# Context attention and layer kernel: prologue in another order, W turned in it, residuals in three steps, VectorE splits the layer's first three units

## The reference

```python
# 1: attention to the context, one W for queries and output
trans_q = einsum('bqh,oh->bqo', ctx, W) + b
att = softmax(einsum('bph,bqh->bpq', layernorm(x), trans_q))
x = x + relu(einsum('bph,oh->bpo', einsum('bpq,bqh->bph', att, ctx), W) + b)
# 2: a layer of linear attention (wq, wk, wv, wo, 16 heads) and a gelu MLP
# 3: a mixture of 8 gated experts, two of them for each token
```

## Time and profile before

| | us |
|---|---|
| runs | 699.74, 931.4, 698.71 (median 699.74) |
| profiled execution, its own time | 702.32 |
| its span, first to last instruction | 700.6 |
| TensorE busy | 651.6 |
| VectorE busy | 426.5 |
| ScalarE busy | 372.8 |
| POOL busy | 252.9 |
| mean granted TensorE clock | 0.968 |

### The profile page before, as it was taken

How to read it: one execution, slowest core, us unless ns; L and a number is a source line. 1 busy time by engine, 2 the same in 40 slices (tenths; PEclk the granted TensorE clock), 3 DMA queues, 4 the chain that set the end, 5 groups by cost and what they waited for, 6 DMA issues and landing times.

```text
span 700.6 us, 9558 instructions
## 1 busy us (share of the span) xinstructions
PE 651.6 (93%) x3370; PEld 538.0 (77%) x3371; DVE 426.5 (61%) x688; ACT 372.8 (53%) x523; POOL 252.9 (36%) x172
## 2 busy tenths in 40 slices
PE   4979998998998999989969999969999999999994
PEld 4868886886876788878758888768888888888883
DVE  8566666656677545576776354845475463762775
ACT  4499986986973254430142244322574555754850
POOL 5078885776894424340000022123022020220233
PEclk9999998998999999999989999969999999999998
DMA  8435453343041612221080793316599191991925
GB/s 324 187 120 175 148 182 129 121 138 118 9 143 60 198 61 90 83 98 62 1 279 22 242 403 120 120 46 238 182 353 373 53 360 46 356 371 66 341 84 176
DMA packets 51844, 116.95 MB, mean 167 GB/s; under 512 B 5208, under 2 KB 5208, under 8 KB 48736
## 3 DMA queue, kind: packets, MB, share of 16 engines
q1 hardware_dynamic: 47360, 106.51, 43.2%
q10 hardware_dynamic: 3168, 5.77, 2.4%
q0 software_dynamic: 1280, 4.20, 1.8%
HBM read 102.31 MB, written 14.16 MB: 166 GB/s over the span
## 4 chain that ended last, share of the span: by engine, by line
PE 78%; DVE 12%; ACT 3%; issue 3%; DMA 2%; POOL 1%; SPq 0%; POOLq 0%; DVEq 0%; ACTq 0%
PE bank L1351 18%; PE bank L1353 18%; PE bank L1352 18%; PE bank L1365 5%; PE bank L1416 3%; PE bank L1417 3%; PE bank L1384 3%; PE bank L1385 3%; PE bank L1750 1%; PE bank L1580 1%; PE bank L1401 1%; PE bank L1730 1%; PE bank L1568 1%; DVE xn L984 1%; PE bank L1737 1%
## 5 line engine op out<-in xcount | busy, mean ns | idle before, releaser
L466 POOL TENSOR_TENSOR nat_lo<-raw,nat_hi 128x512 fp32r<-128x512 f32 x104 | 134.3, 1315 | 55.9 <-ACT nat_hi L584 55.3
L515 POOL TENSOR_TENSOR e_lo<-e_raw,e_hi 128x2048 fp32r<-128x2048 f32 x9 | 41.6, 4619 | 230.2 <-ACT e_hi L743 230.2
L863 DVE TENSOR_TENSOR ct_lo<-bank,ct_hi 128x512 fp32r<-128x512 f32 x96 | 65.9, 689 | 48.7 <-ACT ct_hi L551 48.4
L1351 PE MATMUL bank<-w_hi,turned 128*128 128x512 f32 x176 | 70.7, 402 | 4.0 <-DVE turned L990 2.6
L551 ACT ACTIVATE ct_hi<-bank 128x512 fp32r<-128x512 f32 x96 | 57.1, 596 | 26.4 <-PE bank L1365 24.5
L1352 PE MATMUL bank<-w_lo,turned 128*128 128x512 f32 x176 | 69.5, 395 | 0.0
L1353 PE MATMUL bank<-w_hi,turned 128*128 128x512 f32 x176 | 69.4, 394 | 0.0
L584 ACT ACTIVATE nat_hi<-raw 128x512 fp32r<-128x512 f32 x104 | 65.0, 629 | 0.0
L1365 PE MATMUL bank<-ident,raw 128*128 128x128 f32 x384 | 61.1, 285 | 0.0
L1351 PE MATMUL bank<-e_hi,turned 128*128 128x512 f32 x144 | 59.0, 409 | 1.5 <-issue 1.5
L1365 PEld LDWEIGHTS bank<-ident,raw 128*128 128x128 f32 x384 | 50.1, 147 | 12.7 <-issue 1.2
(11 more groups left out here) (252 smaller groups left out, 1449.8 us busy)
## 6 DMA issues: line engine op xcount, KB each, us to landing
raw<-in_ctx_dram SPq DMA_DIRECT2D x24, 1024.0 KB, 5.0
w_raw<-in_L_ffn_w_dram SPq DMA_DIRECT2D x24, 1024.0 KB, 5.4
e_raw<-in_L_ffn_wo_dram SPq DMA_DIRECT2D x16, 1024.0 KB, 7.4
w_raw<-in_L_attn_w_dram SPq DMA_DIRECT2D x8, 1024.0 KB, 5.2
e_raw<-in_L_ffn_w_dram SPq DMA_DIRECT2D x8, 1024.0 KB, 7.4
slots_x<-zeros SPq DMA_DIRECT2D x1, 4096.0 KB, 16.9
slots_y<-zeros SPq DMA_DIRECT2D x1, 3840.0 KB, 26.2
vectors<-slots_x ACTq DMA_DIRECT2D x11, 256.0 KB, 5.0
```

Source lines behind the costliest of these rows:

```text
L466: nc.gpsimd.tensor_tensor(nat_lo[:, j, :], raw[b % 2][:, j, :], nat_hi[:, j, :].bitcast(f32), ALU.subtract).then_inc(nat_lo_ready, 1)
L515: nc.gpsimd.tensor_tensor(e_lo[j][:, :, :], e_raw[j][:, :, :], e_hi[j][:, :, :].bitcast(f32), ALU.subtract).then_inc(e_lo_ready[j], 1)
L863: nc.vector.tensor_tensor(ct_lo[:, n % CR, :], src, ct_hi[:, n % CR, :].bitcast(f32), ALU.subtract).then_inc(t_lo, 1)
L1351: nc.tensor.matmul(dst, lh, rh, start=first and k == 0, stop=False)
```

## The change

Four things, none of which changes what is computed.

1. The prologue's order. VectorE normalises the first two token tiles before the statistics of the fourth, and POOL waits for pn before its W_lo. TensorE does the first token product ahead of the first three context tiles, with its four W_hi x pnT_hi matmuls first.
2. W is turned between the token products, in bank VB[1] alone, and not in steps 4 to 10. The nat copies begin in step 8 instead of 6 and catch up with three in step 18 (values_at).
3. The residual is output_taken at its old step 41, the sum at step 45 and the statistics at 46 (after the batch pair's odd batch b, step 13 b + 41 and so on); for the third pair all of it comes after the loop.
4. Units 0, 1 and 2 are all split by VectorE, the first as the first thing behind the loop; value product 2 comes ahead of the turning of xn's third tile.

```diff
@@ rules and POOL
+        def values_at(s):
+            if s < 18:
+                return range(s - 8, s - 7) if s >= 8 else range(0)
+            return range(10, 13) if s == 18 else range(s - 6, min(s - 5, B * NKT))
...
+            pool.wait_ge(pn_ready, NT)
             for k in range(KD // 2, KD):
                 pool.wait_ge(W_hi_ready, k + 1)
...
-            split_w(1)
             first_roots(3)
-            split_w(2)
@@ ScalarE
-                if s in (4, 6, 8, 10):
-                    upper_WT(s // 2 - 2)
...
-                if 0 <= s - 6 < B * NKT:
-                    upper_values((s - 6) // NKT, (s - 6) % NKT)
+                for i in values_at(s):
+                    upper_values(i // NKT, i % NKT)
@@ VectorE, prologue
+            link(statistics((0, 1)))
+            variances(0)
+            last = statistics((2,))
+            tokens(0)
+            link(statistics((3,)))
+            variances(1)
+            lower_W(0)
+            tokens(1)
+            lower_W(1)
...
+            lower_pw(0)
             for n in range(3):
                 lower_context(n)
...
+            for m in range(1, KD):
+                lower_WT(m - 1)
+                lower_pw(m)
+                lower_context(2 + m)
+            lower_WT(KD - 1)
@@ VectorE, loop
-                    if b % 2 == 1 and s == G * b + (41 if b < B - 3 else 45):
+                    if b % 2 == 1 and b < B - 3 and s == G * b + 41:
+                        output_taken(b // 2)
+                    if b % 2 == 1 and b < B - 3 and s == G * b + 45:
                         residual(b // 2)
+                    if b % 2 == 1 and b < B - 3 and s == G * b + 46:
                         dve.wait_ge(x1_ready, b // 2 + 1)
                         first_stats(b // 2)
@@ VectorE, behind the loop
             split_w(0)
             lower_turned(0)
+            sum_values(B - 1)
             lower_turned(1)
-            sum_values(B - 1)
-            first_gained(2)
+            output_taken(NT - 2)
+            residual(NT - 2)
             lower_vectors(NT - 1)
+            dve.wait_ge(x1_ready, NT - 1)
+            first_stats(NT - 2)
+            split_w(1)
+            first_gained(NT - 2)
+            output_taken(NT - 1)
             residual(NT - 1)
...
+            split_w(2)
@@ TensorE
+            pe.wait_ge(pnT_hi_ready, NT)
+            pe.wait_ge(pnT_lo_ready, 1)
+            for k in range(KD):
+                pe.wait_ge(W_hi_ready, k + 1)
+                nc.tensor.matmul(bank[3][:, :], W_hi[:, k, 0:P], pnT_hi[:, k, :], start=k == 0, stop=False)
...
             for n in range(3):
                 context_turned(n)
...
+            for m in range(1, KD):
+                turned_W(m - 1)
+                token_product(m).then_inc(pwT_done, 1)
+                context_turned(2 + m)
+            turned_W(KD - 1)
...
             value_product(1)
             for k in range(KD):
                 projected_out(NT - 1, k)
+            value_product(2)
             tile_turned(2)
-            for n in range(2, 5):
+            for n in range(3, 5):
                 value_product(n)
```

More of the change, by code:

```diff
@@ L614, in upper_pn @@
                                      ACT.Copy).then_inc(pnT_hi_ready, 1)
-            for k in range(KD - 1):
-                upper_W(k)
+            upper_W(0)
+            upper_W(1)
             upper_pn(0)
-            upper_W(KD - 1)
-            for t in range(1, NT):
+            upper_W(2)
+            upper_pn(1)
+            upper_W(3)
+            for t in range(2, NT):
                 upper_pn(t)
+            upper_pw(0)
             for n in range(3):
                 upper_context(n)
-            upper_context(3)
-            upper_pw(0)
-            upper_context(4)
-            upper_pw(1)
-            upper_context(5)
-            upper_pw(2)
-            upper_pw(3)
+            for m in range(1, KD):
+                upper_WT(m - 1)
+                upper_pw(m)
+                upper_context(2 + m)
+            upper_WT(KD - 1)
             def split_w(u):
@@ L925, in bias_part, with statistics, variances @@
                     last.then_inc(pb_done, 1)
-            for half in range(2):
-                for t in (2 * half, 2 * half + 1):
+            def statistics(tiles):
+                for t in tiles:
                     dve.wait_ge(x_loaded[t], 16)
                     last = nc.vector.bn_stats(stats[:, t, :], xt[:, t, :])
-                link(last)
+                return last
+            def variances(half):
                 for t in (2 * half, 2 * half + 1):
@@ L1435, in turned_W, with token_product @@
             def turned_W(k):
-                pe.wait_ge(pw_lo_ready, KD)
-                if k >= 2:
-                    pe.wait_ge(WT_lo_ready, k - 1)
+                if k >= 1:
+                    pe.wait_ge(WT_lo_ready, k)
                 for m in range(KD):
-                    mm = nc.tensor.transpose(VB[k % 2][:, m * P:(m + 1) * P], Wn[:, m, k * P:(k + 1) * P], ident[:, :])
+                    mm = nc.tensor.transpose(VB[1][:, m * P:(m + 1) * P], Wn[:, m, k * P:(k + 1) * P], ident[:, :])
                 mm.then_inc(WT_done, 1)
+            def token_product(m):
+                return product(bank[3 + m][:, :], [(W_hi[:, k, m * P:(m + 1) * P], W_lo[:, k, m * P:(m + 1) * P]) for k in range(KD)],
+                               [(pnT_hi[:, k, :], pnT_lo[:, k, :]) for k in range(KD)])
             pe.wait_ge(const_ready, 1)
```

52 lines of the change are left out of this document (21 added, 31 removed).

## The result

| | before | changed |
|---|---|---|
| median of the runs | 699.23 us (698.71 without 931.4) | 690.87 us |
| runs | 697.96, 698.71, 699.74, 931.4 | 688.31, 689.71, 692.02, 692.91 |
| profiled execution: time, span | 702.32, 700.6 | 692.91, 691.1 |
| its granted clock, mean | 0.968 | 0.972 |

The ratio is 0.9884, with a 95% interval from 0.9845 to 0.9923. The change makes the kernel 1.2% faster (0.8 to 1.6%): 8.1 us by the ratio and 7.8 to 8.4 by the medians, where 17.8 were forecast. (The run of before at 931.4 us stands alone and is left out of the ratio; why it was slow is not known.)

A forecast was written before the change was run, and what follows sets the result against it. TensorE, busy 651.6 of 700.6 us, was taken as the bound, improvable only in idle and low-clock time. Gains 11.2 + 2.1 + 1.2 + 3.3 = 17.8 us gave 681.9 us, range 678 to 692.

The forecast's parts named there:

- Residual in three steps: In the batch loop: VectorE frees pT sooner, TensorE's two long waits fall to 0 to 0.3 us; gain 11.2 us.
- The second payment: In the batch loop: low-clock time behind each long pT wait, 3.1 of the 5.7 us that one wait costs.
- The base: Whole kernel: profiled 702.32 us less 17.8 gives 684.5; the median run lies 2.6 lower, so 681.9.
- Prologue and start of the loop: Before and in the first thirteen steps: score step 2.1 us earlier, then 1.2 us from three steps at the high level.
- its worse case: In the prologue: the first token product runs at the low level, taking 5.3 us instead of 2.8.
- The wait of 1.9 that was to stay: At the loop's start: TensorE still waits 1.9 us before its score step, with no clock fall behind it.
- the 1.2: At the loop's start: three steps take 3.3 us at the high level instead of 4.48; 0 if the level falls.
- Layer's first units: Behind the loop: VectorE splits unit 0 first and units 1 and 2 too; gain 3.3 us (1.5 to 4.5).
- the case in which VectorE issues first: Behind the loop: VectorE's unit 0 split gets in before POOL's last nat_lo, which ends at 211.6; gain 2.7 us.
- The second: Rival: start and tail give little (low-level first product, fall behind the remaining wait, VectorE first); gain 13.8, 685.9 us; chance 0.18.
- The first: Rival: the low level does not hang on the waits and comes elsewhere; only waits count, 8.8 us, 690.9 us; chance 0.12.
- the pace: Sign in the batch loop: the fourth and fifth batches' turnings lie 19.3 to 19.8 us apart.

The follow-up runs named there:

- e13: Kernel before with 9 products of a zero tile ahead of TensorE's pT waits in the fourth and sixth batch: 696.7 us, ratio 0.9969.
- e2: Kernel before with only the new start (statistics and token order, weight splits, first product, W turned in the prologue, natural values): 700.7 us, ratio 1.0003.
- e4: Changed kernel with the old start put back, residuals in three steps and new tail kept: 689.8 us, ratio 0.9854 to before.
- e6: Changed kernel with identity turnings added: 32 ahead of the first tokens, 8 between their pairs, 6 ahead of the first product: 686.3 us, ratio 0.9838 to before.
- e11: Changed kernel with ScalarE's natural values 2 to 5 moved to steps 12 and 13, two at a time: 691.8 us, ratio 0.9893 to before.
- e12: Changed kernel with warm start, ScalarE's unit 1 behind the last lower values, earlier first mask and later values 2 to 5: 681.9 us, ratio 0.9751 to before.
- e3: Kernel before with only the new tail (units 0 to 2, order of sums behind the loop, third value product): 698.7 us, ratio 0.9977.
- e8: Changed kernel with ScalarE's unit 1 split and its nat_lo wait behind the turned second tile and last lower values: 689.3 us, ratio 0.9866 to before.
- e14: e12 with identity turnings added, 26 ahead of the wait for the chosen experts, 12 ahead of the first expert's rows: 686.7 us, ratio 0.9816 to before.
- e5: Kernel before with 24 identity turnings in batches b = 4 and 6, behind the batches that wait for pT: 704.9 us, ratio 1.0076.

## Why the prediction was wrong

The sign and the mechanism of the largest term were right; all four terms were too large, and two of them came to nothing.

- **Residual in three steps, 11.2 us (ends 4.8 and 11.6): 6.9 alone.** This is the step that failed most, by 4.3 us, and it is a size. The three steps do free pT (waits of 2.6 us to none; fourth to fifth batch 19.6 us, as said), and each of the two waits did cost 2.5. The second payment, 3.1 us per wait, is what the profiled execution had; in the runs it is 1.1 on the mean (e13: 2.2 for both, interval 0.2 to 4.2). The sentence "so each long wait is paid twice" should have read: sometimes, and by different amounts.
- **The base.** 702.32 was carried to the median by taking off 2.6. But that execution lost more at the low level than most (22.4 us at a clock of 0.968, as much as the highest of the 21 runs of before above), and a part of that very loss was the gain that was forecast. It can't be won by the change and be left out of the base too.
- **Prologue and start of the loop, 2.1 + 1.2 us: nothing** (e2: 1.0003; e4). The loop began at 30.63, outside the 27.5 to 30.0. The first product ran at half the rate, which the prediction named as its worse case (5.3 us; it was 5.1) and did not take; e6 shows that this alone is 2.05 us, nearly all of the 2.1 that the loop was late. That it was still slow then is put down here to the gaps that the new order puts ahead of it (1.25 and 0.69 us), where before worked from 8.22 to 14.1 us without one; e6 filled the gaps and added 32 turnings ahead of the tokens at once, so this cause is argued and not shown apart. The wait of 1.9 that was to stay is 1.60, and behind it the level fell in five of the seven profiles that have it, so the 1.2 was mostly lost too (18.3 us from the loop's start to the first probabilities with the fall, 17.3 without). Where the wait is 0.66 (e11, e12) no fall followed.
- **Layer's first units, 3.3 us (4.1 or 2.7): 2.45** in the trace, 1.6 in the runs (e3, interval -0.5 to 3.7). VectorE got in first. Its split starts 0.07 us ahead of GpSimd's last subtraction, which takes 3.36 us, where its like in before took 1.29, and ends at 200.24; ScalarE, which waits for it, is late for the last lower values. By the rule of the Trainium skill, page "SBUF — State Buffer", section "Who interferes with whom", this is the case in which VectorE issues first, with 2.7, and the 3.36 agrees with it. No xn takes 5 us any more (1.67 at most), since GpSimd has no split beside it. That unit 1 would be in the way of the last sum on ScalarE was in the prediction's working, but not as something that an order could mend; e8 takes 1.4 us from it.
- **Rivals.** The second described the start and the tail as they came (low level through the first product, loop at 30.0 or later, a fall behind the wait that stays, VectorE first), but kept 11.2 for the residual and so named 685.9. The first named the very time, 690.9, but that is luck: its 8.8 us held 2.1 for the start, which gave nothing, and e13 speaks against its claim that the level doesn't hang on the waits, for the waits for pT. What it had right is that the level falls elsewhere too, at a place where before had shown none. That 690.9 lies within the range of 678 to 692 is owed to these two rivals alone; the forecast's own gains ended at 14, and a gain under 2% had a chance of 0.26.
- **What would show it.** Met: no 2.6 us for pT, the pace, 1.00 from 50 to 200 us, no xn of 5 us. Not met: the loop's start, the first probabilities (48.94, not 45.4), av only 1.7 us nearer the last probabilities. Neither condition for being wrong came true as it was written (no wait over 2.5 us at a new place, no low level in the batches from 50 to 200 us). What took 4.7 us in the profile was a place that neither looked at: 0.51 for 14 us in the attention, behind a wait of 1.42.

Open stays why the level falls in one execution and not in the next behind the same wait, and why all four runs of e11 lost over 17 us. Where the level fell in executions without a profile is not on record, only the sum over each.

## What to carry to other kernels

Split a gain into the wait, which every execution has, and the low clock behind it, which comes and goes: read the latter over several executions (span x (1 - clock) of each, as an upper bound), never from one profile. Before a first long product, and through a wait that can't be removed, turnings of the identity into a free bank are a cheap way to keep TensorE fast, but they help only if they fit: at a low level they outlast the wait and are late themselves (e14). And when an instruction that must wait stands on an in-order engine, look at what is queued behind it (here unit 1's split ahead of the last lower values) before counting what the new order gives.

## What the runs showed of the hardware

- The loss at the low level comes in steps: 1.7, 3.4 or 6.8 us at one place, whatever the wait. At the fourth batch's wait of 2.56 us it was 3.4 in before, 1.7 in e5 and 0 in e3, which run the same instructions up to there. Behind the wait of 2.54 to 2.58 us in the layer's start it was 1.7 in each of five profiles.
- At the start TensorE works at half its rate while the granted clock reads 1.00: eight turnings take 1.94 us at 7.04 in after, and 1.11 at 7.97 in e6, where the filler had gone ahead. In e6 itself the first turnings start 0.21 us apart, and from 4.6 us on 0.11. In after the rate stays low up to 17.5 us, over two gaps (1.25 and 0.69). The granted clock alone would have missed it.
- A loss is not the time that a fall costs. In the attention 6.8 us of loss cost 4.7 us (14.8 instead of 10.1), behind the wait for mx 1.7 us of loss cost 1.0 up to the first probabilities.
- Behind the wait of 1.42 us in the attention, which is the same in twelve profiles, the loss went from 0 to 6.8. Whether a fall comes, and how long it is, does not follow from the wait alone.
- GpSimd's writings of rows to slots_x take 0.96 to 1.23 us each, but 1.90 to 4.98 where they start beside VectorE's two splits of 2.28 us (after, e8, e12, e14).
